# Routing of the batches earlier, scatters given out by step, late layer norms on VectorE, and the maxima turned at the end of a step

## The chip, the cores and the metric

One core of a Trainium2 chip runs the whole program. The metric is the device time of one execution in microseconds (us). Engines are named as in the profile: PE (matrix products), DVE (vector), ACT (activations), POOL (GpSimd), SP (the queue that issues most transfers).

## The reference, cut to what matters

Eight batches of 256 tokens with 256 features go through one cross-attention layer (16 heads of 16 features) and one mixture-of-experts layer (8 experts, hidden size 1024, two experts for each token), in float32:

```python
x = x + xattn(layernorm(x), ctx, ctx, Wq, Wk, Wv, Wo, bo, masks)     # softmax(q k' / 4) v, then Wo
z = layernorm(x)
gate = softmax(z @ w_gate.T);  two largest per token, their weights in cw
h = gelu(einsum('td,edh->teh', z, W1) + b1)
x = x + einsum('ted,te->td', einsum('teh,ehd->ted', h, W2) + b2, cw)
```

The kernel computes an expert only for the tokens that chose it. It writes each token's normalised row twice, into the lists of its two experts, and later works through these lists.

## The kernel before, in words

**Steps.** All engines run the same list of steps, s = -16 to 99, each engine its own part of each step in a fixed order. Nothing but semaphores ties the engines together, so "step" is an order on each engine and no clock. Step s takes one pair of heads (m = s mod 8) of batch n = s div 8 through the first score product: `scores_for_max(s)` on PE, then the row maxima `nmax` on DVE (`take_max`, L863). Ten steps later the same pair is multiplied again with the maximum subtracted (`scores(s - 10)`, L1341) and exponentiated on ACT (L1143); `weighted` (L1353) multiplies two such pairs by the values in every other step. So the 64 instructions L863 lie in steps 0 to 63 and the 64 instructions L1143 in steps 10 to 73. In this way rows of the trace are given step numbers here.

**The table of due steps.** What happens once per batch hangs on names in a table `due[s]`: for the back of the attention `div`, `divide`, `ao`, `aT`, `o`, `add`, then the second layer norm `ln2` (statistics, DVE), `norm2` (POOL: the power -0.5 of the variance, `inverse_deviation`, L554, and the two normalising instructions, L565), `y` (four turns on PE), `yT` (ACT). The routing follows in six groups of batches, (0, 1), (2, 3), 4, 5, 6 and 7: `logits` (PE), `choose` (DVE), `gate_exp` (ACT), `gates`, `tags` (DVE), `count` (PE), `places`, `rows` (DVE) and `scatter` (POOL). A scatter is one indirect DMA (L575) for each half batch and each of two choices: eight for a group of two batches and four for one of one. `total` (PE) sums the counts after groups 3, 4 and 5, and `lists_of` (DVE) makes the table of tiles from it. POOL's `scatter` waits for the group's `rows` and `tags` and then issues its DMAs without another wait.

**The maxima.** Row maxima of one batch are put together on DVE in step 8n+7 (`maxima`), turned on PE at the very start of step 8n+8 (`turn_maxima`, L1294), copied by ACT to `mT` (L1102) and sent by ACT's DMA queue (L1124) into the operand of `scores`. In ACT's own order `maxima_out` is the first thing of step 8n+8, ahead of that step's exponential.

**The experts.** From step 76 on each step also holds a unit, a quarter of a tile. 23 tiles (16 of 256 rows, 7 of 128) are worked through: gather of the rows, two weight matrices of 1 MB each, split in two parts by ACT and DVE, 48 + 48 products for a full tile on PE, the scaled sum on DVE and an indirect add to the output on POOL (L534). SP loads a tile's rows (`xg`) and weights in `sp_tile`; tiles 0 and 1 are loaded in step 71, behind the first table and behind the landings of the scatters of groups 0 to 3. After step 99 the units go on by themselves.

## Time and profile before

| what | value |
|---|---|
| median of 3 runs | 527.25 us (525.56 to 530.07) |
| the profiled execution | 525.33 us, of which the span from first to last instruction is 524.0 us |
| PE busy | 457.9 us, 87% of the span |
| DVE, ACT, POOL busy | 69%, 64%, 32% |
| mean granted PE clock | 0.94 of full |

The page shows shares of the whole span. The kernel has quite different stages, though: attention at an even pace up to about 177 us, a mixed stage to about 241 us, and the experts from there to the end. What matters is read from the stage in question.

### The profile page before, as it was taken

Reading aid. Unit: us, or ns where it says so; the run is one execution under the profiler, and the core shown is the slowest. Engines: PE = TensorE matmul, PEld = TensorE weight load, DVE = VectorE, ACT = ScalarE, POOL = GpSimd, SP = SyncE. Lnnn points to the kernel's source line nnn. Section 1 sums busy time; section 2 is a strip of 40 time slices with the busy share of each in tenths; the row PEclk is TensorE's granted clock in tenths of the full one; section 3 lists DMA queues with packets and bytes.
Section 4 is the critical chain, followed back from the end, with each engine's and each line's share of the span. In section 5 each row is a group of like instructions: output and inputs, shape, how many; then the busy total and the mean of one; then the engine's idle time right before and its main releaser. Section 6 shows DMA issues by size and latency. Waiting matters only on the chain.

```text
span 524.0 us, 10489 instructions
## 1 busy us (share of the span) xinstructions
PE 457.9 (87%) x3741; PEld 390.5 (75%) x3741; DVE 360.4 (69%) x791; ACT 334.8 (64%) x569; POOL 165.2 (32%) x213
## 2 busy tenths in 40 slices
PE   4897989999999844658889987999999999999993
PEld 3365666766765622427889977899999999999992
DVE  3276776776777751336977997298868788888862
ACT  1123776667666522335968856498779889889880
POOL 6023330352321577210361513132333213312323
PEclk9999999999999966665989989899999999999998
DMA  6557615324310023149275859859787987878822
GB/s 226 175 159 218 210 62 171 124 69 150 124 66 24 31 95 106 42 164 357 83 246 176 278 154 269 254 206 270 218 242 240 277 250 232 276 266 245 282 32 30
DMA packets 44356, 93.03 MB, mean 178 GB/s; under 512 B 6928, under 2 KB 30096, under 8 KB 38416
## 3 DMA queue, kind: packets, MB, share of 16 engines
q1 hardware_dynamic: 35072, 81.41, 46.3%
q0 software_dynamic: 7152, 9.46, 9.3%
q10 hardware_dynamic: 2080, 1.49, 0.9%
q8 instruction: 31, 0.51, 0.4%
q14 instruction: 21, 0.17, 0.1%
HBM read 63.01 MB, written 14.26 MB: 147 GB/s over the span
## 4 chain that ended last, share of the span: by engine, by line
PE 52%; issue 10%; DVE 10%; ACT 9%; DMA 6%; POOL 4%; another core or an unknown queue 4%; SPq 3%; ACTq 1%; DVEq 0%; POOLq 0%
PE S L1218 13%; PE bank L1233 12%; PE bank L1278 6%; PE bank L1286 5%; PE S L1318 4%; DMA w_in<-in_W 4%; PE bank L1353 3%; DVE nmax L863 3%; ACT hf L1068 2%; PE S L1391 2%; PE bank L1270 2%; PE S L1341 2%; ACT W2p L1049 2%; ACT Q L1037 1%
## 5 line engine op out<-in xcount | busy, mean ns | idle before, releaser
L1218 PE MATMUL S<-xgT,Q 128*128 128x256 f32 (+1 forms) x736 | 139.1, 289 | 8.7 <-DVE xgT L757 5.2
L534 POOL DMA_INDIRECT out<-y,slot x39 | 69.4, 1780 | 177.3 <-DVE y L781 103.7
L1218 PEld LDWEIGHTS S<-xgT,Q 128*128 128x128 f32 x736 | 117.5, 198 | 9.3 <-issue 9.3
L863 DVE TENSOR_REDUCE nmax<-S 128x4 f32<-128x1024 f32 x64 | 78.4, 1225 | 47.6 <-PE S L1318 45.1
L1218 PE MATMUL S<-xgT,K 128*128 128x256 f32 (+1 forms) x368 | 105.6, 287 | 0.0
L1068 ACT ACTIVATE hf<-S,b1c 128x256 f32<-128x256 f32 (+1 forms) x184 | 70.6, 435 | 40.2 <-PE S L1218 36.4
L1143 ACT ACTIVATE prob<-S 128x1024 f32<-128x1024 f32 x64 | 65.8, 1028 | 38.8 <-PE S L1341 27.7
L767 DVE TENSOR_TENSOR hp<-hf,hp 128x512 fp32r<-128x512 f32 (+1 forms) x92 | 55.8, 607 | 29.7 <-ACT hp L1081 29.3
L1218 PEld LDWEIGHTS S<-xgT,K 128*128 128x128 f32 x368 | 72.6, 197 | 0.0
L734 DVE TENSOR_TENSOR K<-w_in,Q 128x1024 fp32r<-128x1024 f32 x46 | 56.4, 1225 | 19.9 <-ACT Q L1037 19.9
L1233 PE MATMUL bank<-W2p,hp 128*128 128x256 f32 x528 | 67.6, 284 | 0.3 <-DVE y L777 0.3
L1233 PEld LDWEIGHTS bank<-W2p,hp 128*128 128x128 f32 x528 | 64.7, 191 | 0.6 <-issue 0.4
L554 POOL TENSOR_TENSOR rstd<-ve,half 128x2 f32<-128x2 f32 x16 | 11.8, 736 | 137.7 <-DVE ve L848 137.3
L1081 ACT ACTIVATE hp<-hf 128x512 fp32r<-128x512 f32 (+1 forms) x92 | 52.3, 569 | 2.9
L1037 ACT ACTIVATE Q<-w_in 128x1024 fp32r<-128x1024 f32 x46 | 48.2, 1048 | 8.6 <-DMA w_in<-in_W 7.5
L1233 PE MATMUL bank<-Q,hp 128*128 128x256 f32 x272 | 51.3, 282 | 1.3 <-DVE y L777 1.2
L1233 PEld LDWEIGHTS bank<-Q,hp 128*128 128x128 f32 x272 | 42.9, 188 | 1.6 <-issue 1.6
L575 POOL DMA_INDIRECT lists<-x2n,rows x32 | 31.7, 990 | 39.3 <-DVE rows L965 31.1
L1353 PE MATMUL bank<-prob,V 128*32 128x256 f32 x512 | 37.7, 416 | 1.2 <-ACT prob L1143 1.2
L1233 PE MATMUL bank<-K,hp 128*128 128x256 f32 x136 | 38.3, 282 | 0.0
L1318 PEld LDWEIGHTS S<-K,Q 64*128 64x128 f32 x256 | 19.1, 184 | 24.8 <-issue 13.2
L1318 PE MATMUL S<-K,Q 64*128 64x256 f32 x256 | 32.2, 330 | 5.7 <-DVE nmax L863 5.1
(179 smaller groups left out, 702.1 us busy)
## 6 DMA issues: line engine op xcount, KB each, us to landing
w_in<-in_W SPq DMA_DIRECT2D x46, 1024.0 KB, 7.9
K<-flat_k SPq DMA_DIRECT2D x24, 256.0 KB, 2.4
Q<-flat_q SPq DMA_DIRECT2D x24, 256.0 KB
xg<-lists SPq DMA_DIRECT2D x16, 265.0 KB
b_in<-in_b SPq DMA_DIRECT2D x23, 128.0 KB
lists<-zero SPq DMA_DIRECT2D x9, 265.0 KB, 4.9
cin<-in_ctxT SPq DMA_DIRECT2D x8, 256.0 KB, 3.5
xin<-in_x SPq DMA_DIRECT2D x8, 256.0 KB, 3.9
```

The source lines that it names most:

```text
L534: st_y[i % 4].after(pool.indirect_dma_start(out=out, out_offset=bass.IndirectOffsetOnAxis(ap=slot[i % 4][:, t:t + 1], axis=0), in_=y[i % 2 ...
L734: w1_lo.after(dve.tensor_tensor(W1p[i % 2][1][:, c], w1_in[i % 2][:, c], W1p[i % 2][0][:, c].bitcast(F32), ALU.subtract))
L767: h_lo.after(dve.tensor_tensor(hp[i % 2][1][:, c, 0:n], hf[pair % 2][:, :, 0:n], hp[i % 2][0][:, c, 0:n].bitcast(F32), ALU.subtract))
L863: max_done.after(dve.tensor_reduce(nmax[n % 4][:, :, :, m].rearrange("p t r -> p r t"), S1[:].rearrange("p r (t k) -> p r t k", t=TT), AX. ...
L1037: w1_hi.after(act.activation(W1p[i % 2][0][:, c], w1_in[i % 2][:, c], ACT.Copy))
L1068: h_act.after(act.activation(hf[pair % 2][:, u, 0:n], h_bank[pair][:, u, 0:n], ACT.Gelu, bias=b1c[i % 3][:, 2 * pair + u:2 * pair + u + 1]))
L1081: h_hi.after(act.activation(hp[i % 2][0][:, 2 * pair:2 * pair + 2, 0:n], hf[pair % 2][:, :, 0:n], ACT.Copy))
L1143: exp_done.after(act.activation(prob[s % 4][:].rearrange("p r t l -> p (r t l)"), S2[:].rearrange("p r l -> p (r l)"), ACT.Exp, scale=SCALE))
L1218: ins = pe.matmul(h_bank[pair][:, u, 0:n], W1p[k][a][:, kc, m * P:(m + 1) * P], xgT[k][c][:, kc, 0:n], start=(j == 0), stop=(j == len(term ...
L1233: ins = pe.matmul(y_bank[:, t, :], hp[k][a][:, m, t * P:(t + 1) * P], W2p[k][c][:, m, :], start=(j == 0), stop=(j == len(terms) - 1))
L1318: i = pe.matmul(S1[:, r, t * L:(t + 1) * L], Q[n % HELD][a, m, t * P:(t + 1) * P], K[n % HELD][a, m, :], start=not masked, stop=(not maske ...
L1353: i = pe.matmul(b[j * OS:(j + 1) * OS, 0:L], V[n % 3][:, t, r * MP + m, :], prob[(MP * n + m) % 4][:, r, t, :], start=(t == 0), stop=(t == ...
```

## The change

- `ROUTE` now gives each group its own steps. Group 0: `rows` in step 51, 60 before. Group 1: `rows` in 61, 63 before. Group 2: 64, 65 before. Group 3: 68, 69 before. Group 4: 78, 77 before. Group 5 keeps 89. In the early groups a DVE part that reads a PE result stands one step behind it (`count` 59, `places` 60), where before both could be in one step.
- `scatter` no longer stands in the table: `SCATTERS` gives each group a first step and a number of DMAs for each step (1 for group 0, 2 for groups 1, 2 and 4, 4 for groups 3 and 5). Only the first DMA of a group waits.
- Batches 3 to 7 have their two normalising instructions of the second layer norm on DVE, under a due name of their own, `norm_dve`; before, DVE had them only for batch 6. POOL keeps `inverse_deviation`.
- `turn_maxima` stands behind `scores_for_max`, `scores`, `div` and `weighted` of its step on PE. ACT's order isn't changed.
- `total` of stage 0 and the loads of tiles 0 and 1 are one step sooner (69 and 70).

```diff
+    ON_DVE = 3
+    SCATTERS = {0: (51, 1), 1: (61, 2), 2: (65, 2), 3: (69, 4), 4: (78, 2), 5: (90, 4)}
-    ROUTE = dict(logits=38, choose=39, gate_exp=40, gates=42, tags=46, count=50, places=51, rows=52, scatter=54)
     LATE_BACK = {
-        4: dict(div=52, divide=53, ao=54, aT=55, o=57, add=58, store=59, ln2=59, norm2=59, y=61, yT=62),
-        5: dict(div=59, divide=59, ao=60, aT=61, o=61, add=62, store=63, ln2=62, norm2=63, y=64, yT=65),
-        6: dict(div=67, divide=67, ao=68, aT=69, o=69, add=70, store=71, ln2=71, norm2=71, y=72, yT=73),
-        7: dict(div=77, divide=77, ao=79, aT=79, o=81, add=81, store=83, ln2=81, norm2=82, y=84, yT=84)}
-    LATE_ROUTE = {
-        1: dict(logits=60, choose=60, gate_exp=61, gates=62, tags=62, count=62, places=62, rows=63, scatter=63),
-        2: dict(logits=63, choose=63, gate_exp=64, gates=65, tags=65, count=65, places=65, rows=65, scatter=66),
-        3: dict(logits=66, choose=66, gate_exp=67, gates=68, tags=68, count=68, places=69, rows=69, scatter=70),
-        4: dict(logits=74, choose=74, gate_exp=75, gates=76, tags=76, count=76, places=76, rows=77, scatter=78),
-        5: dict(logits=86, choose=86, gate_exp=88, gates=88, tags=88, count=89, places=89, rows=89, scatter=90)}
-    LISTED = {0: (3, 70), 1: (4, 79), 2: (5, 92)}
+        3: dict(div=44, divide=45, ao=46, aT=47, o=50, add=51, store=53, ln2=52, norm2=52, norm_dve=53, y=54, yT=55),
+        4: dict(div=52, divide=53, ao=54, aT=55, o=56, add=57, store=59, ln2=57, norm2=57, norm_dve=58, y=59, yT=60),
+        5: dict(div=59, divide=60, ao=61, aT=61, o=62, add=63, store=64, ln2=63, norm2=63, norm_dve=64, y=65, yT=65),
+        6: dict(div=67, divide=67, ao=68, aT=69, o=69, add=70, store=71, ln2=70, norm2=70, norm_dve=71, y=73, yT=74),
+        7: dict(div=77, divide=77, ao=79, aT=79, o=81, add=81, store=83, ln2=81, norm2=82, norm_dve=82, y=84, yT=84)}
+    ROUTE = {
+        0: dict(logits=45, choose=46, gate_exp=47, gates=48, tags=48, count=49, places=50, rows=51),
+        1: dict(logits=56, choose=57, gate_exp=58, gates=59, tags=59, count=59, places=60, rows=61),
+        2: dict(logits=61, choose=62, gate_exp=63, gates=63, tags=63, count=63, places=64, rows=64),
+        3: dict(logits=66, choose=66, gate_exp=67, gates=68, tags=68, count=68, places=68, rows=68),
+        4: dict(logits=75, choose=75, gate_exp=76, gates=76, tags=76, count=77, places=77, rows=78),
+        5: dict(logits=86, choose=86, gate_exp=88, gates=88, tags=88, count=89, places=89, rows=89)}
+    LISTED = {0: (3, 69), 1: (4, 79), 2: (5, 92)}
...
-        SP_TILES = {71: (0, 1), 76: (2,), 79: (3,), 82: (4,), 86: (5,), 90: (6,)}
+        SP_TILES = {70: (0, 1), 76: (2,), 79: (3,), 82: (4,), 86: (5,), 90: (6,)}
...
-                    if now["norm2"] != NB - 2:
+                    if now["norm2"] < ON_DVE:
                         normalise(1, now["norm2"])
-                if "scatter" in now:
-                    scatter(now["scatter"])
+                for i, (first_step, each) in SCATTERS.items():
+                    for k in range(each):
+                        scatter(i, (s - first_step) * each + k)
...
+                if "norm_dve" in now:
+                    normalise(1, now["norm_dve"])
...
-                if "mx" in now:
-                    turn_maxima(now["mx"])
                 if 0 <= s < NP:
                     scores_for_max(s)
                 if 0 <= s - LAG < NP:
@@ -1412,6 +1415,8 @@
                 n, m = divmod(s - LAG - 2, MP)
                 if 0 <= n < NB and m % 2 == 0:
                     weighted(n, m // 2)
+                if "mx" in now:
+                    turn_maxima(now["mx"])
```

## Rows read from the trace of the kernel before

**Rows 1.** Table of stretches of the span: busy time, granted clock, DMA share.

```profile
101.40:122.10 20.70, 20.05 (x184) 13.93 (x183) 15.11 (x30) 14.23 (x21) 7.66 (x8) 1.00 0.36 121
...
204.00:236.00 32.00, 17.01 (x122) 9.86 (x122) 9.54 (x52) 10.02 (x16) 9.82 (x11) 0.61 0.29 105
...
270.00:274.00 4.00, 4.00 (x23) 4.00 (x22) 1.28 (x4) 2.72 (x5) 2.55 (x2) 0.57 0.91 280
```

**Rows 2.** Timeline: exponentials of steps 60 and 69, first expert product.

```profile
175.44 1.03 ACT L1143 ACTIVATE prob<-S 128x1024 f32<-128x1024 f32 x1 [0.80 <-PE S L1341]
...
219.76 1.02 ACT L1143 ACTIVATE prob<-S 128x1024 f32<-128x1024 f32 x1
...
241.74 0.77 PE L1218 MATMUL S<-xgT,Q 128*128 128x256 f32 x2 [1.73 <-DVE xgT L757]
```

**Rows 3.** Chain that ended last, 177 to 242 us: four of its pieces.

```profile
185.40 4.19 another core or an unknown queue
...
198.79 4.33 another core or an unknown queue
...
204.17 8.87 another core or an unknown queue
...
222.65 2.52 another core or an unknown queue
```

**Rows 4.** Timeline of group 0's first scatter, steps 62 and 63, and of steps 66 and 67.

```profile
181.00 1.23 POOL L575 DMA_INDIRECT lists<-x2n,rows  x1 [0.34 <-DVE rows L965]
...
185.14 0.50 PE L1318 MATMUL S<-K,Q 64*128 64x256 f32 x4
...
192.52 1.02 ACT L1143 ACTIVATE prob<-S 128x1024 f32<-128x1024 f32 x1 [6.83 <-remote]
...
201.38 1.19 PE L1370 MATMUL bank<-WgT,yT 128*128 128x8 f32 x8
...
213.16 0.17 DVE L917 TENSOR_SCALAR gate<-bank 128x16 f32<-128x16 f32 x1 [11.70 <-remote]
```

**Rows 5.** Timeline: last scatter of the second run, and group 4's last.

```profile
209.82 0.96 POOL L575 DMA_INDIRECT lists<-x2n,rows  x1 [0.30 <-issue]
...
254.36 0.97 POOL L575 DMA_INDIRECT lists<-x2n,rows  x1 [0.31 <-issue]
```

**Rows 6.** Timeline of step 32, in which the maxima of batch 3 are turned.

```profile
101.72 0.38 PE L1294 MATMUL bank<-ident,mrep 128*32 128x128 f32 x2
...
102.19 0.38 ACT L1102 ACTIVATE mT<-bank 32x256 f32<-32x256 f32 x1 [1.17 <-PE bank L1294]
...
102.60 0.64 ACTq L1124 DMA_DIRECT2D Q<-mT  x1
102.70 1.07 PE L1353 MATMUL bank<-prob,V 128*32 128x256 f32 x16
...
103.34 1.03 ACT L1143 ACTIVATE prob<-S 128x1024 f32<-128x1024 f32 x1 [0.77 <-PE S L1341]
...
105.67 1.99 PE L1278 MATMUL bank<-xT,WqT 128*128 128x256 f32 x8 [0.65 <-ACT xT L1102]
```

**Rows 7.** Timeline: normalising of batches 4, 6 and 7.

```profile
180.72 0.66 PE L1270 MATMUL bank<-ident,x2n 128*128 128x128 f32 x4 [1.28 <-POOL x2n L565]
...
230.66 0.74 DVE L854 TENSOR_SCALAR x2n<-x,mv,rstd 128x256 f32<-128x256 f32 x2 [0.94 <-POOL rstd L554]
...
264.25 4.75 POOL L565 TENSOR_SCALAR x2n<-x,mv,rstd 128x256 f32<-128x256 f32 x2
...
269.05 0.66 PE L1270 MATMUL bank<-ident,x2n 128*128 128x128 f32 x4 [1.90 <-POOL x2n L565]
```

**Rows 8.** Timeline: group 3's rows, total 0, and the first load of rows.

```profile
219.06 0.16 DVE L965 TENSOR_REDUCE rows<-off 128x2 int32<-128x16 f32 x1
...
223.28 0.18 PE L1395 MATMUL bank<-run,onesb 128*128 128x8 bf16 x1
...
230.30 0.41 SPq L383 DMA_DIRECT2D xg<-lists  x1
```

More of the change, by code:

```diff
@@ L136, in build @@
             due[LATE_BACK[n][name] if n in LATE_BACK else MP * n + o][name] = n
+        if n in LATE_BACK:
+            due[LATE_BACK[n]["norm_dve"]]["norm_dve"] = n
     for i, ns in enumerate(GROUPS):
-        for name, o in ROUTE.items():
-            due[LATE_ROUTE[i][name] if i in LATE_ROUTE else MP * ns[-1] + o][name] = i
+        for name, step in ROUTE[i].items():
+            due[step][name] = i
     for stage, (i, step) in LISTED.items():
@@ L559, in normalise @@
                     pool.wait_ge(pe_misc.sem, filled_by("xn", n - 1))
-                if which and n >= KEPT:
-                    pool.wait_ge(pe_misc.sem, filled_by("y", n - KEPT))
-                    pool.wait_ge(st_list[n % KEPT].sem, 16 * TT * TOP * (n // KEPT))
                 for t in range(TT):
@@ L566, in normalise, with scatter @@
                                                            ALU.subtract, ALU.mult))
-            def scatter(i):
+            def scatter(i, d):
                 ns = GROUPS[i]
-                pool.wait_ge(rows_done.sem, 2 * (i + 1))
-                pool.wait_ge(x2n_tag.sem, 2 * (i + 1))
-                for u, n in enumerate(ns):
-                    for t in range(TT):
-                        for k in range(TOP):
-                            st_list[n % KEPT].after(pool.indirect_dma_start(
-                                out=lists, out_offset=bass.IndirectOffsetOnAxis(
-                                    ap=rows[i % 2][:, k, u * TT + t:u * TT + t + 1], axis=0),
-                                in_=x2n[:, n % KEPT, t], in_offset=None))
+                if not 0 <= d < len(ns) * TT * TOP:
+                    return
+                u, t, k = d // (TT * TOP), d // TOP % TT, d % TOP
+                if d == 0:
+                    pool.wait_ge(rows_done.sem, 2 * (i + 1))
+                    pool.wait_ge(x2n_tag.sem, 2 * (i + 1))
+                n = ns[u]
+                st_list[n % KEPT].after(pool.indirect_dma_start(
+                    out=lists, out_offset=bass.IndirectOffsetOnAxis(
+                        ap=rows[i % 2][:, k, u * TT + t:u * TT + t + 1], axis=0),
+                    in_=x2n[:, n % KEPT, t], in_offset=None))
             pool_r.after(pool.memset(taken[:], 0.0))
@@ L851, in normalise @@
                 dve.wait_ge(ln_rstd[which].sem, n + 1)
+                if which and n >= KEPT:
+                    dve.wait_ge(pe_misc.sem, filled_by("y", n - KEPT))
+                    dve.wait_ge(st_list[n % KEPT].sem, 16 * TT * TOP * (n // KEPT))
                 for t in range(TT):
@@ L993, in dve_attention @@
                     statistics(1, now["ln2"])
-                    if now["ln2"] == NB - 2:
-                        n = now["ln2"]
-                        dve.wait_ge(pe_misc.sem, filled_by("y", n - KEPT))
-                        dve.wait_ge(st_list[n % KEPT].sem, 16 * TT * TOP * (n // KEPT))
-                        normalise(1, n)
+                if "norm_dve" in now:
+                    normalise(1, now["norm_dve"])
                 if "ln1" in now:
```

## The prediction

> **What bounds the kernel now.** I read the table of stretches first, since the page's shares mix three stages. In attention at its even pace eight steps take 20.7 us, and PE is busy in 20.05 of them at the full clock (2.4 GHz) [rows 1]: PE bounds it, and what holds PE there costs its full length. Between 204 and 236 us no engine is busy for much more than half the time and the mean granted clock is 0.61, mostly the lower level (1.2 GHz) [rows 1]. In the timeline steps 60 to 69 take 219.76 - 175.44 = 44.3 us, 4.9 us each, where 2.6 was the pace, and the first expert product starts at 241.74 [rows 2]. From there on tile follows tile; SP, POOL and DVE do their parts unit by unit, so what starts the first tile sooner ends the kernel sooner by the same.
>
> The chain of waits tells what stretches steps 60 to 73: four pieces that it puts down to no engine of this core, 4.19, 4.33, 8.87 and 2.52 us, 19.9 in all [rows 3]. The timeline is to be read for what PE had done by then. PE's products of step 63 are recorded from 185.14 on, yet the exponential fed by them starts at 192.52; the logits of group 3 are recorded at 201.38, yet DVE reads them at 213.16, after 11.70 us of waiting [rows 4]. So PE's completions arrive late, not its work. In that time POOL issues scatters back to back, 0.96 us each with 0.30 between: eight from 181.00 on, to 191.1, and twelve up to 209.82 + 0.96 = 210.8 [rows 4, 5]. The late completions come from about the fourth scatter of a run on, and stop some 1 to 2.5 us after its last. The four of group 4, ending at 255.3 [rows 5], hold nobody. I take the length of a run of scatters as the cause; the trace shows only that they go together. A page would allow the lateness itself: the Trainium skill (Perfetto Trace Analysis, Tensor Engine Instruction) says that a product's recorded end is estimated and that its semaphore goes out only when PSUM has acknowledged the bytes.
>
> Counted against the pace of the neighbouring steps, the lateness costs 4.3 us in the run of eight (steps 62 to 64), 9.6 in the run of twelve (64 to 67) and 1.5 in group 3's four: 15.4 of the 19.9, because other work went on beside it.
>
> **The change part by part.**
>
> Maxima turned at the end of the step. Removed: 0.31 us of PE ahead of the scores. But ACT copies the turned maxima first in its step, and its exponential comes behind. In step 32 now: turn at 101.72, copy at 102.19 (0.47 later, 0.38 long), DMA issue at 102.60 for 0.64, exponential at 103.34 [rows 6]. With the change the turn stands behind `weighted`, which would start 0.33 sooner, at 102.37, and takes 1.00: turn at 103.37, copy 103.85, issue 104.27, exponential 105.0. That is 1.66 us later. PE needs this exponential for the next scores, and the turned rows that ACT copies behind it for the q products at 105.67, for which it waits 0.65 already [rows 6]. Between them it has only 0.7 us of other work. So PE loses 1.66 us in each of steps 16, 24, 32, 40 and 48, and perhaps 0.5 in step 56, where 3.9 us of `o` and `logits` products fill the hole: +8.8. Nothing gives this back, as PE bounds the stage. Ends: 0 (if DVE or the queue order hides all of it) and 6 x 1.66 = 10.
>
> Routing sooner. Its work isn't less, only moved: of group 1's some 2.9 us of DVE and 1.9 of PE (the same instructions in the timeline before) leave steps 60 to 63 for 56 to 60. Beside PE-bound steps it is paid there and saved later: 0. Its ends are -2 and +3 us: at best PE's holes hide it, at worst DVE becomes the bound of 57 and 58.
>
> DVE readers one step behind. When PE's completion is late by less than a step, DVE no longer stands still with `nmax` queued behind the reader; but the scores wait on late completions all the same. I take -1 us; ends 0 and -3.
>
> Scatters given out. Here the code decides: POOL has no clock of steps. After the first DMA of a group only other waits of POOL's part them. Group 0: one, then the wait for `ln2` of batch 3, then five in a row, then that of batch 4, then two. Group 1: four, the wait for `ln2` of batch 5 in step 63, then four; group 2's `rows` (step 64) are ready before these end (4 x 1.26 = 5 us, two steps), so its four follow at once: a run of eight. Group 3: four. In place of 8, 12 and 4 the runs are 5, 2, 4, 8 and 4. Priced as now, a run of four at 1.5 to 2, of five 2.5 (it has one scatter beyond the fourth), of eight 4.3: 2.5 + 2 + 4.3 = 8.8 ahead of group 3's, where 4.3 + 9.6 = 13.9 are lost now: -5.1. Ends: -13.9 (no run is late) and 0.
>
> Norms on DVE. For batches 3, 4, 5 and 7 DVE gets 0.74 us and POOL loses 2.4 or more. The wait of PE for batch 4, 1.28 us [rows 7], goes: -1.3. Batch 7: POOL took 4.75 us, and PE stood 1.90 [rows 7]; the clock then fell and was 0.57 in the next 4 us [rows 1], worth 1.7 (half of the 3.4 us at the lower level). Next due is DVE, whose order has two units' work ahead, so both go: -3.6; ends -2 and -4.5. If DVE were the bound there, its 0.74 would come back. The added wait is DVE's for `rstd`: behind it in step 64 stands `nmax` of no further step, but `choose` and `rows`; behind it in 58 `nmax` of step 59. POOL's `inverse_deviation` stands behind up to five scatters, 6.3 us. By the order above these are issued before DVE has the variance; I take 0, the other end is the last rival.
>
> First table a step sooner. From group 3's `rows` (219.06) to the load of its tile's rows (230.30) are 11.2 us now [rows 8]. The scatters take 4 x 1.26 = 5.0 and land about 2 us later, 7 in all; the table's small DVE instructions and SP's register loads take 230.30 - 223.28 = 7.0 behind `total`, which came 4.2 behind `rows` [rows 8] and with its step brought forward can come right behind them. So 7.2 in place of 11.2: -4.0. Ends -5 and -1. The 11.4 us from this load to the first product [rows 2, 8] stay (5.0 of them are the weights' transfer), and the exponentials of steps 69 to 73 fit beside them at 2.6 each.
>
> Clock. PE is busy for 17.0 us between 204 and 236 at a mean clock of 0.61 [rows 1]; at the full clock the same products would take 10.4. With fewer holes part of these 6.6 us comes back, but much of it lies beside waits: I take -1.5, ends 0 and -4.
>
> Group 4 and 5, and the store of batch 6 that now stands behind two tile loads on SP, end beside the experts: 0.
>
> **Sum**, against the profiled execution: 8.8 - 1.0 - 5.1 - 1.3 - 3.6 - 4.0 - 1.5 = -7.7, so 525.3 - 7.7 = 517.6 us. This execution lies 1.9 below the median of the runs and 0.2 below their lowest; I put the median at 519.
>
> **Rivals.**
>
> The runs don't stall at all any more, since none but one is longer than five. For it: group 4's four cost nothing. Against: the run of eight is left. It gives 519 - 8.8 = 510.
>
> The maxima cost nothing. Against it speaks that ACT's order has no way round. For it: PE's record ends are modelled, and its 97% may hide slack that takes up 1.7 us in each eight steps. It gives 510 as well, and 501 with the first.
>
> The scatters are not the cause, or each costs the same 0.64 us (15.4 / 24) however it is dealt: the change doesn't do what it says. All 13.9 us stay: 519 + 5.1 = 524, or with the other gains at their weak ends 526. The Trainium skill (SBUF — State Buffer, two separate sides) has a rule for this: PE's port waits for nobody, and transfers and engine ports don't contend. By that rule scatters could not hold PE; rows 4 show them together, and nothing else that would.
>
> Slower: DVE waits for POOL. `norm_dve` of batches 4, 5 and 6 needs `rstd`, which POOL computes only when its scatters ahead are issued, and all of DVE's queue stands behind. It decides from the point where a group's `rows` come less than 5.0 us (four scatters) before `ln2` of the next batch; group 1's are due two steps, 5.5 us, before. Once each with 5 us, and with the stalls as they are now: 519 + 5.1 + 2 x 5 = 534.
>
> **How the numbers follow.** Forecast, 519 (513 to 523): 0.45. No stalls, 510: 0.17. Free maxima, 510 or less: 0.13. Stalls unchanged, 524 to 526: 0.15. DVE behind POOL, 534: 0.10. The range takes both cases of 510 with part of what lies below, and those of 524 to 526 with 1 us more: 503 to 527. Changes under 1% (5.3 us) can hardly be told from none with this kernel, whose runs differ by 4.5 us. Faster by more (under 522): four fifths of the first case and the next two, 0.66; slower (over 532.5): 0.10; the rest, 0.24, is the same.
>
> **What would show it.** In the attention stage eight steps should take 22.3 us and the exponential of step 32 start 3.3 us after the turn's old place. Runs of scatters in the timeline: 1, 5, 2, 4, 8, 4. The pieces of the chain without an engine should add up to some 10 us, the largest in the run of eight. From group 3's `rows` to the load 7 us; first product at about 235 to 238; no fall of the clock at batch 7's turns. I am wrong if the even stage keeps 20.7 us (maxima), if late completions appear without POOL's scatters or stay away in the run of eight, or if DVE idles before L854 for several us.

## The result and the profile after

The changed kernel takes 545.38 us (median of 4 runs, 544.59 to 546.95); the kernel before took 527.62 us beside it (525.56 to 530.07). The ratio is 1.037 (95% interval 1.032 to 1.042): slower by 18 us, where 8 us less were forecast. The profiled execution took 544.59 us, its span is 543.3 us; lines after L150 stand 4 to 8 further down than before. The page of the changed kernel, busy time and granted clock in 40 slices of 13.6 us:

```profile
PE 470.4 (87%) x3741; PEld 399.2 (73%) x3741; DVE 363.1 (67%) x799; ACT 333.7 (61%) x569; POOL 155.4 (29%) x205
...
PE   4898898998978878775799988599999999999993
...
PEclk9999998989899866667799999799999999999998
```

PE's share of the span is the 87% of before, but that is 470.4 us busy in place of 457.9 for the same 3741 instructions, which last longer at the lower clock. The clock's line of the page of the kernel before, in slices of 13.1 us, for comparison:

```profile
PEclk9999999999999966665989989899999999999998
```

Now the clock falls again and again from slice 7 on, and from 186 to 248 us its mean is 0.61. The same in the table of stretches (busy time of PE, PEld, DVE, ACT and POOL with counts, granted clock, DMA share, GB/s): first the eight steps from the exponential of step 24 to that of step 32, then two pieces of step 32, then about steps 57 to 73.

```profile
84.30:107.80 23.50, 21.33 (x178) 14.60 (x178) 15.22 (x30) 13.59 (x20) 4.81 (x6) 0.93 0.33 107
107.80:111.20 3.40, 1.56 (x9) 1.25 (x10) 0.91 (x1) 3.19 (x5) 2.85 (x3) 1.00 0.12 26
111.20:114.60 3.40, 3.40 (x21) 2.10 (x23) 0.95 (x1) 1.12 (x2) 0.00 (x0) 0.51 0.00 0
...
186.00:248.00 62.00, 48.88 (x332) 32.88 (x332) 30.37 (x121) 22.19 (x33) 19.58 (x21) 0.61 0.19 64
```

Steps 24 to 32 now take 23.50 us; the same steps took 20.33 before (exponentials at 83.01 and 103.34). The cause is in the timeline of step 32 (start, duration, engine, line; in brackets the wait ahead and who ended it), which answers to [rows 6]:

```profile
106.18 0.39 PE L1299 MATMUL bank<-ident,mrep 128*32 128x128 f32 x2
...
106.67 0.37 ACT L1107 ACTIVATE mT<-bank 32x256 f32<-32x256 f32 x1 [2.95 <-PE bank L1299]
...
107.81 1.02 ACT L1148 ACTIVATE prob<-S 128x1024 f32<-128x1024 f32 x1 [0.77 <-ACT mT L1107]
...
108.89 0.50 PE L1346 MATMUL S<-Q,K 64*128 64x256 f32 x4 [1.45 <-ACT prob L1148]
...
110.14 2.31 PE L1283 MATMUL bank<-xT,WqT 128*128 128x256 f32 x7 [0.75 <-ACT xT L1107]
```

ACT stands still for 2.95 us until PE has turned the maxima; the exponential comes 1.14 us behind the copy, and PE waits for it (1.45) and again for the turned rows (0.75). Then comes what I had not counted: from 111.2 to 114.6 us the granted clock is at the lower level (0.51, so 1.2 of 2.4 GHz), and eight q products whose records took 1.99 us [rows 6] last from 110.14 to about 112.8 (the last row shows seven of the eight). The clock falls so in steps 24, 32 and 40. In step 16 PE has the same two waits, 1.45 and 0.75 us, and the q products still take 2.00 us: no fall there. From exponential to exponential each of the four turns costs 1.77 us (step 32 comes 5.11 behind step 31, where it was 3.34), and each of the three falls 1.4 to 1.6 more: 4 x 1.77 + 4.5 = 11.6 us.

The chain's pieces without an engine, 19.9 us in [rows 3], are down to two:

```profile
225.96 2.38 another core or an unknown queue
228.38 2.85 another core or an unknown queue
```

And from group 3's rows to the load of the first tile's rows and to the first product, which answers to [rows 8] and the last of [rows 2]:

```profile
236.96 0.16 DVE L973 TENSOR_REDUCE rows<-off 128x2 int32<-128x16 f32 x1
...
244.11 0.41 SPq L388 DMA_DIRECT2D xg<-lists  x1
...
257.21 0.77 PE L1223 MATMUL S<-xgT,Q 128*128 128x256 f32 x2 [4.09 <-DVE xgT L762]
```

7.15 us where 11.24 were, but then 13.1 to the product in place of 11.4.

The two kernels by stage, cut at the starts of exponentials, at the first expert product and at DVE's split of the fifth tile's rows (tile 4; L757, now L762), us. The right half is a later series of runs (last experiments), in which the kernel before took only 512.8 us:

| stage | before | changed | difference | before, later | changed, later | difference |
|---|---|---|---|---|---|---|
| to step 15 | 60.06 | 57.81 | -2.3 | 59.81 | 58.91 | -0.9 |
| 15 to 45 | 76.62 | 88.22 | +11.6 | 76.59 | 88.25 | +11.7 |
| 45 to 54 | 24.58 | 28.94 | +4.4 | 26.25 | 28.93 | +2.7 |
| 54 to 62 | 22.56 | 34.86 | +12.3 | 25.17 | 34.43 | +9.3 |
| 62 to 72 | 43.35 | 35.48 | -7.9 | 25.02 | 31.38 | +6.4 |
| 72 to first product | 14.57 | 11.90 | -2.7 | 16.10 | 14.74 | -1.4 |
| to tile 4 | 51.17 | 52.15 | +1.0 | 49.49 | 52.16 | +2.7 |
| to the end of the span | 231.09 | 233.94 | +2.9 | 230.87 | 231.40 | +0.5 |
| span | 524.0 | 543.3 | +19.3 | 509.3 | 540.2 | +30.9 |

The stage to step 15 lasted 57.5 to 60.1 us in all traces whatever the kernel, and single stages between 45 and 72 shift by 1.5 to 2.5 us among kernels that do the same work there; smaller differences mean nothing. The last stage too lasted 230.3 to 233.0 us among kernels with the expert code of before. The 25.02 of steps 62 to 72 is the lowest of its kind: the kernels of runs 11, 13 and 14, with the same work there or nearly so, took 28.5 to 29.7 in the later series, and 22.0 to 23.5 in steps 54 to 62, where this trace has 25.17.

### The profile page after: what moved, and what is told of

It reads as the page before. It is cut to its first block, busy times and chain, and to the rows that moved or that the text cites. A ratio compares the mean times of both kernels' runs of the same rounds, so it can differ in the third digit from the quotient of the medians.

```text
span 543.3 us, 10488 instructions
## 1 busy us (share of the span) xinstructions
PE 470.4 (87%) x3741; PEld 399.2 (73%) x3741; DVE 363.1 (67%) x799; ACT 333.7 (61%) x569; POOL 155.4 (29%) x205
## 4 chain that ended last, share of the span: by engine, by line
PE 60%; DVE 11%; ACT 10%; issue 8%; DMA 5%; SPq 2%; POOL 2%; another core or an unknown queue 1%; ACTq 1%; DVEq 0%; POOLq 0%
PE S L1223 16%; PE bank L1238 13%; PE bank L1283 6%; PE bank L1291 5%; PE bank L1358 5%; PE S L1323 5%; DVE nmax L871 3%; DMA w_in<-in_W 3%; PE S L1346 3%; ACT hf L1073 2%; PE S L1396 2%; PE bank L1275 2%; ACT Q L1042 2%; ACT prob L1148 1%; PE bank L1375 1%
## 5 line engine op out<-in xcount | busy, mean ns | idle before, releaser
L1223 PEld LDWEIGHTS S<-xgT,Q 128*128 128x128 f32 x736 | 116.5, 196 | 12.4 <-issue 12.3
L539 POOL DMA_INDIRECT out<-y,slot x39 | 71.5, 1833 | 179.1 <-DVE y L786 92.1
L1042 ACT ACTIVATE Q<-w_in 128x1024 fp32r<-128x1024 f32 x46 | 48.1, 1046 | 13.6 <-DMA w_in<-in_W 13.5
L1086 ACT ACTIVATE hp<-hf 128x512 fp32r<-128x512 f32 (+1 forms) x92 | 52.2, 567 | 2.9
L1346 PE MATMUL S<-Q,K 64*128 64x256 f32 x256 | 31.3, 327 | 16.3 <-ACT prob L1148 14.4
L1323 PEld LDWEIGHTS S<-K,Q 64*128 64x128 f32 x256 | 21.0, 202 | 31.9 <-issue 16.1
L1323 PE MATMUL S<-K,Q 64*128 64x256 f32 x256 | 34.7, 352 | 10.7 <-DVE nmax L871 10.4
L1358 PE MATMUL bank<-prob,V 128*32 128x256 f32 x512 | 39.0, 428 | 2.5 <-DVE ao L900 1.9
```

What stands on the lines that cost most here:

```text
L539: st_y[i % 4].after(pool.indirect_dma_start(out=out, out_offset=bass.IndirectOffsetOnAxis(ap=slot[i % 4][:, t:t + 1], axis=0), in_=y[i % 2 ...
L1042: w1_hi.after(act.activation(W1p[i % 2][0][:, c], w1_in[i % 2][:, c], ACT.Copy))
L1086: h_hi.after(act.activation(hp[i % 2][0][:, 2 * pair:2 * pair + 2, 0:n], hf[pair % 2][:, :, 0:n], ACT.Copy))
L1223: ins = pe.matmul(h_bank[pair][:, u, 0:n], W1p[k][a][:, kc, m * P:(m + 1) * P], xgT[k][c][:, kc, 0:n], start=(j == 0), stop=(j == len(term ...
L1323: i = pe.matmul(S1[:, r, t * L:(t + 1) * L], Q[n % HELD][a, m, t * P:(t + 1) * P], K[n % HELD][a, m, :], start=not masked, stop=(not maske ...
L1358: i = pe.matmul(b[j * OS:(j + 1) * OS, 0:L], V[n % 3][:, t, r * MP + m, :], prob[(MP * n + m) % 4][:, r, t, :], start=(t == 0), stop=(t == ...
```

## The experiments

"On before" and "on changed" say which kernel was edited. Times are medians, the ratio is to the kernel before in the same series. There are four series of four runs each, and each ran on another chip: runs 1 to 4 on number 0, 5 to 8 on 10, 9 to 12 on 15 and 13 to 16 on 5. A piece of the chain without an engine is a wait for something that the profile can't name; a single instruction's wait of this kind is marked `remote`.

**1. Maxima at the start again, on changed.** The call of `turn_maxima(now["mx"])` moved back ahead of the scores.

> The changed kernel with one part undone: the maxima are turned at the start of their step on PE again. Theory M (the turn's place costs all of the loss, because ACT's exponential waits behind the copy, PE stands still and its clock falls in each batch): eight steps take 20.7 us again instead of 24, the exponential of step 60 comes near 183 us instead of 200.5, and the time is 520 to 527. Theory R (the routing steps and the norms on DVE cost it): the time stays above 538, and steps 48 to 60 stay slow.

529.92 us, 1.010 (1.005 to 1.016): 15.5 us less than the changed kernel. Stage 15 to 45 is 76.61 us again. But 54 to 62 stays at 33.3 us, where before had 22.6: a second loss that has nothing to do with the maxima.

**2. Maxima at the end alone, on before.**

```diff
-                if "mx" in now:
-                    turn_maxima(now["mx"])
                 if 0 <= s < NP:
...
                     weighted(n, m // 2)
+                if "mx" in now:
+                    turn_maxima(now["mx"])
```

> The kernel before with one part of the change alone: the maxima are turned behind the weighted sums of their step. Theory M: 3.3 us lost in each of five steps and some in step 56, the exponential of step 60 at 192 instead of 175, a time of 540 to 547. Forecast of the prediction for this part: +8.8, so 536. Theory R: no more than 3 us above the kernel before.

539.29 us, 1.027 (1.021 to 1.033), +14.5 us; 15 to 45 takes 88.56 us, so 11.9 more for four batches: 3.0 each on average, of which 1.77 is the wait; the clock falls behind steps 24, 32, 40 and 56, not behind 16 and 48. Step 56 pays the full 1.78 as well. From both sides the late turn costs about 15 us.

**3. ACT's exponential first, on changed.** `maxima_out` put behind `exponentials` on ACT; PE still turns late.

> The changed kernel with the maxima still turned at the end of the step on PE, but ACT takes its copy of them behind the step's exponential instead of ahead of it. Theory M with ACT's order as the mechanism: PE no longer waits for the exponential, eight steps take 20.4 to 21 us, the time is within 3 us of the kernel with the turn at the start (520 to 527). If PE's own order is what costs (the bank, or the later transfer of the maxima), the time stays above 535.

534.92 us, 1.019 (1.014 to 1.024). Stage 15 to 45 takes 79.80 us: of the 11.6 us there 8.4 are gone. Step 32 there:

```profile
102.12 1.02 ACT L1148 ACTIVATE prob<-S 128x1024 f32<-128x1024 f32 x1 [1.57 <-PE S L1346]
...
103.01 0.39 PE L1299 MATMUL bank<-ident,mrep 128*32 128x128 f32 x2
...
103.50 0.37 ACT L1107 ACTIVATE mT<-bank 32x256 f32<-32x256 f32 x1 [0.35 <-PE bank L1299]
...
105.35 0.60 ACT L1107 ACTIVATE xT<-bank 128x512 f32<-128x512 f32 x1
...
106.00 1.99 PE L1283 MATMUL bank<-xT,WqT 128*128 128x256 f32 x8 [1.50 <-ACT xT L1107]
```

The exponential waits for its scores alone, the q products take 1.99 us again, and the clock is granted in full (1.00) from step 16 to 45; what is left, 0.8 us for each batch, is PE's 1.50 for the turned rows, where it waited 0.65 [rows 6]. ACT's order is the main mechanism, and the fall of the clock behind it carries a good part of the price. The time stays 5.0 us above run 1, though, and not within the 3 that I had expected: besides the 3.2 of this stage, steps 45 to 54 take 29.29 in place of 27.62, with a fall of the clock behind step 48.

**4. Scatters spaced out, on before.** Each scatter of groups 0 to 2 waits until the one before has landed.

```diff
                         for k in range(TOP):
+                            if i < 3:
+                                pool.wait_ge(st_list[n % KEPT].sem, st_list[n % KEPT].value)
```

> The kernel before, but each scatter of groups 0 to 2 waits on POOL until the one before has landed, so one comes every 3 us or so instead of every 1.26. Theory D (PE's completions come late because scatters are issued back to back): the pieces without an engine in the chain between 180 and 215 us (17.4 us before) fall under 4, and steps 62 to 67 take under 22 us instead of 33.8; the time is 512 to 527, the gain being eaten in part by later landings of the lists. Theory N (each scatter costs 0.64 us however it is spaced, or something else holds PE): the pieces add up to 10 or more again.

545.55 us, 1.039 (1.034 to 1.044). Not one piece of the chain is without an engine and no wait is `remote`, so PE's completions are in time when the scatters stand apart; run 2, on the same chip with the scatters as before, has 20.8 us of such pieces. The price is another one: POOL's queue blocks. The list of waits (engine, line, waited for; us in all, times, longest), 196 to 250 us:

```profile
POOL lists L575 <- DMA lists<-x2n,rows: 27.7, 15, 2.1
...
PE bank L1272 <- DVE x2n L856: 19.2, 1, 19.2
...
PE bank L1272 <- POOL x2n L565: 16.1, 1, 16.1
```

The norms behind the scatters on POOL come late and PE stands for 19.2 and 16.1 us. It says nothing of what the stalls are worth.

**5. Late norms on DVE, on before** (batches 3, 4, 5 and 7 at steps 57, 60, 63 and 82).

```diff
+    for n, step in {3: 57, 4: 60, 5: 63, 6: 71, 7: 82}.items():
+        due[step]["norm_dve"] = n
...
-                    if now["norm2"] != NB - 2:
+                    if now["norm2"] < 3:
                         normalise(1, now["norm2"])
...
```

> The kernel before with one part alone: batches 3 to 7 have their second layer norm's normalising on DVE, at steps 57, 60, 63, 71 and 82; routing, scatters and maxima as before. The prediction has -1.3 for batch 4 and -3.6 for batch 7: 4.9 us off, about 520 against 525. The rival (DVE waits behind POOL's scatters for the power, with the next maxima queued behind it) expects no gain or a loss of up to 5 us: in step 63 DVE has to wait for POOL, which is issuing eight scatters.

520.65 us, 0.988 (0.980 to 0.996), -5.0 us by the medians, with an interval of about -2 to -10: the fastest of this series. The first product to tile 4 takes 47.37 us in place of 51.17. Part of this isn't the norms' own: the 51.17 holds the fall of the clock at 270 us. Of seven traces with batch 7's norm on POOL and group 4 where it was, two have such a fall (this one and run 4, 51.17 and 51.01); the other five take 49.5 to 50.0 there. DVE waits for `rstd` 1.04 us once, in batch 5.

**6. Scatters in a lump, on changed, maxima at the start.** `SCATTERS = {0: (62, 8), 1: (63, 8), 2: (66, 4), 3: (69, 4), 4: (78, 4), 5: (90, 4)}`.

> The changed kernel with the maxima at the start again and the scatters not given out early: group 0's eight come in step 62 in a row, group 1's eight in 63, group 2's four in 66, group 3's four in 69, with the routing steps as changed. Theory C (the scatters that fell into the PE-bound stage cost more than they saved, because the late completions stop PE there and its clock falls before step 60): steps 48 to 60 take 29 to 31 us instead of 40.3, and the late completions come back after step 62; the time is 518 to 530. Theory W (the routing work itself is what makes steps 48 to 60 slow): they stay at 37 us or more.

532.58 us, 1.012 (1.003 to 1.021), 2.8 us over run 7 of the same series. With runs of 8 and 12 again the chain has only 5.9 us without an engine, but the chain shows too little here: single waits marked `remote` sum to 10.3 us on ACT and 9.7 on DVE, where run 1 has 5.8 and 2.7 and the kernel before 19.1 and 18.5. So the lumps bring part of the lateness back. Steps 54 to 62 take 33.7 us as in run 1. That doesn't clear the scatters: POOL was ahead, group 0's eight ran from 178.2 to 188.3 us, beside the exponentials of steps 58 to 60, and two late completions lie there:

```profile
186.72 1.23 DVE L871 TENSOR_REDUCE nmax<-S 128x4 f32<-128x1024 f32 x1 [3.90 <-remote]
...
188.15 1.02 ACT L1148 ACTIVATE prob<-S 128x1024 f32<-128x1024 f32 x1 [3.57 <-remote]
```

Run 16 settles it: no completion is late there, and these steps take 34.4 us, some 1.5 of it for the late turn. The second loss does not need late completions.

**7. Scatters truly tied to steps, on changed, maxima at the start.** Ahead of each later share of a group POOL waits for `s2_done` of the step.

> The changed kernel with the maxima at the start again, and the scatters of groups 0 to 2 tied to their steps: from a group's second step on POOL waits until the score products of the step before are done. Group 0 then has one scatter every 2.5 us. Theory D (lateness needs scatters back to back): no late completions between 160 and 172 us, where 5 us of chain pieces without an engine or waits for one stood, and steps 48 to 60 take 30 to 33 us instead of 40.3; 518 to 525 in all. Theory N (each scatter costs the same): steps 48 to 60 stay at 38 us or more.

529.75 us, 1.006 (1.002 to 1.011); by the stages as run 1. The waits had mostly been met when POOL came to them, and group 0's scatters still start some 1.3 us apart. It tells nothing of spacing.

**8. First table a step sooner, on before** (group 3's places, rows, scatters, `LISTED` and `SP_TILES` a step sooner).

> The kernel before with one part alone: places and rows of group 3 in step 68, its scatters and the first table in 69, the loads of tiles 0 and 1 in 70. The prediction's term: from group 3's rows to the load 7.2 us instead of 11.2, so 521 against 525. If what stands behind the load (the weights, or the steps up to 76) is what sets the first product, the time stays within 1 us.

524.65 us, 0.995 (0.991 to 0.999): -2.5 us by this ratio, -1.0 by the medians, so a small gain at most. Rows to load fell from 11.2 to 7.2 us, load to first product rose from 11.4 to 13.3.

The next eight ran in two series in which the kernel before took 512.27 and 512.81 us, 12 to 15 less than so far: their times in the expectations are to be read as differences.

**9. Routing of groups 1 and 2 back, on changed, maxima at the start.**

```diff
-    SCATTERS = {0: (51, 1), 1: (61, 2), 2: (65, 2), 3: (69, 4), 4: (78, 2), 5: (90, 4)}
+    SCATTERS = {0: (51, 1), 1: (63, 8), 2: (66, 4), 3: (69, 4), 4: (78, 2), 5: (90, 4)}
...
-        1: dict(logits=56, choose=57, gate_exp=58, gates=59, tags=59, count=59, places=60, rows=61),
-        2: dict(logits=61, choose=62, gate_exp=63, gates=63, tags=63, count=63, places=64, rows=64),
+        1: dict(logits=60, choose=60, gate_exp=61, gates=62, tags=62, count=62, places=62, rows=63),
+        2: dict(logits=63, choose=63, gate_exp=64, gates=65, tags=65, count=65, places=65, rows=65),
...
```

> The changed kernel with the maxima turned at the start and with the routing of groups 1 and 2 (and their scatters) put back to the steps that it had before: norms on DVE, the first table a step sooner and the scatters of groups 4 and 5 dealt out stay. Theory A, the routing of group 1 (two batches) on PE and DVE in steps 56 to 61 is what makes steps 48 to 60 last 40 us in place of 28.7: they fall to 29 to 31 us, steps 60 to 69 grow from 36.2 to 42 to 43 us (as with the norms alone), and the span comes out some 3 to 8 us under the 528.6 of the run without the maxima: 520 to 525. Rival B, the back parts of batches 3 to 5 that the change also moved in these steps (output product, addition, norm) do it: steps 48 to 60 stay at 37 to 40 us and the time at 528 or more.

522.13 us, 1.022 (1.014 to 1.029). Steps 54 to 62 take 25.90 us in place of 33.30, where kernels without the moves take 22.0 to 25.2. Steps 48 to 60, by which I had meant to judge, still take 36.8: they end amid a step that is long in one kernel and short in the other, and were a bad measure. By what was written down neither theory came out: steps 48 to 60 didn't fall to A's 29 to 31, and the time is 10 us over before, where A's 520 to 525 meant 0 to 5 under the 525 that the kernel before then took; B's 37 to 40 us and 3 or more over it were nearly met. What the run does show is the place: steps 54 to 62 lose 7.4 us when groups 1 and 2 go back, though run 1, with which I compare, is of another series. The rest is left: 45 to 54 has +3 and the first product to tile 4 takes 52.2 us. An estimate for the whole: the changed kernel is 29.2 us over before where completions aren't late (run 16), without the late turn (15) it would be some 14 over, and this one is 9.9 over, so putting groups 1 and 2 back gives about 4 us.

**10. Routing of groups 0 and 1 sooner alone, on before** (with batch 3's back part, which it needs).

> The kernel before with the routing of groups 0 and 1 alone moved sooner (group 0 to steps 45 to 51, group 1 to 56 to 61, with the back part of batch 3 that it needs), norms on GpSimd, scatters as before. Theory A: steps 48 to 60 last 36 us or more in place of 28.7, 60 to 69 gives part of it back (44.3 falls to 36 to 40), in all 0 to 6 us slower than before: 525 to 531. Rival B, it is the back parts of batches 4 and 5 and the norms on DVE in these steps: steps 48 to 60 stay under 32 us and the time falls by what 60 to 69 gives back, to 517 to 521.

517.61 us, 1.012 (1.007 to 1.017), +5.3 us by the medians, +6 by the ratio. Steps 54 to 58 take 13.7 us in place of 9.8, steps 48 to 60 33.7: between the two theories. Three things move here. Group 0 alone costs nothing that can be measured (run 14), and batch 3's back part about 1.4 us in steps 49 to 52 (9.5 where run 14 has 8.1), so some 3 to 4 us are left for group 1; no run moves it by itself. That the back parts of batches 4 and 5 in the same steps make it dearer, as the 33.3 us of run 1 suggest, wasn't run alone either.

**11. Norms on DVE and first table sooner together, on before.**

> The kernel before with the two parts together that gained alone: late norms on DVE (5.0 us alone) and the first table a step sooner (2.5 us alone). If they add up: 517 to 519. If both only bring the lists forward and what stands behind them (the last steps before the first unit) sets the end: 519 to 521, as the norms alone.

510.46 us, 0.996 (0.994 to 0.999): -1.8 us here. The norms give their part, 47.37 us to tile 4 (49.49 in run 15). The table gives almost nothing: from group 3's rows to the load are 9.5 us, where run 8 has 7.2 and run 15 10.2. The steps are faster here, so POOL's scatters are what is waited for. Sixteen go out back to back, the last of them starts at 213.67 us, the table is complete at 210.4, and the load comes at 216.43. And DVE, with all its queue, waits twice for POOL's power of the variance, which comes behind the scatters, as the last rival of the prediction had it: 3.63 us at 191.84, behind a run of eight, and here behind the sixteen:

```profile
215.52 0.74 DVE L856 TENSOR_SCALAR x2n<-x,mv,rstd 128x256 f32<-128x256 f32 x2 [3.23 <-POOL rstd L556]
```

Behind tile 4 it takes 232.57 us where run 15 has 230.87; run 14, with the expert code of before, takes 232.96, so that difference says nothing. It is the fastest kernel of these series, as run 5 was of the first; both beat both kernels, by little.

**12. The same with PE turning late and ACT's exponential first.**

> The same as the kernel with norms on DVE and the first table sooner, with the maxima turned at the end of their step on PE, and ScalarE's copy of them put behind its exponential. Theory A, the loss from the late turn is ScalarE's order alone (its exponential queued behind the copy): then this costs nothing beside the kernel with the two parts, 0 plus or minus 2 us. Rival B, the late turn also delays the masked maxima and with them the next batch's query product, or PE's order itself costs: 4 us slower or more.

513.99 us, 1.003 (1.000 to 1.006), 3.5 us over run 11. Stage 15 to 45 takes 79.81 us against 76.62. The 0.8 us for each batch of run 3 stand confirmed, away from the rest of the change: even with ACT's order mended the late turn gains nothing.

**13. Group 4's routing a step later alone, on before** (the changed kernel has it so).

```diff
-        4: dict(logits=74, choose=74, gate_exp=75, gates=76, tags=76, count=76, places=76, rows=77, scatter=78),
+        4: dict(logits=75, choose=75, gate_exp=76, gates=76, tags=76, count=77, places=77, rows=78, scatter=78),
```

> The kernel before with group 4's routing alone one step later, as in the changed kernel (logits and choice in step 75, counts and places in 77, rows in 78). Theory A, PE's count of step 77 stands behind the first unit's products in PE's queue and waits for the choice, which on DVE comes behind the split of the weights and batch 7's division: the stretch from the first unit's first product to the fifth table (tile 4) grows from 51 to 54 to 56 us and the kernel is 3 to 6 us slower than before. Rival B, the 5 us of that stretch come from another of the moves (batch 6's or 7's norm on DVE): 0 plus or minus 1.5 us.

518.37 us, 1.011 (1.007 to 1.015), +5.6 us, as theory A had it; the first product to tile 4 takes 54.26 us in place of 49.49. Its timeline behind the first unit's first products:

```profile
236.03 0.75 DVE L892 TENSOR_TENSOR ao<-bank,rden 128x256 f32<-128x256 f32 x2
236.60 0.17 PE L1385 MATMUL bank<-chosen,before 128*128 128x8 bf16 x1 [3.09 <-DVE ao L892]
...
236.73 0.77 PE L1218 MATMUL S<-xgT,Q 128*128 128x256 f32 x2
```

The counts of step 77, on PE, use a bank that DVE's division of batch 7 must have read first, and DVE comes to that only behind the split of a weight. PE stands 3.09 us with unit 1's products queued behind, and two products still take 0.77 us, their time at the lower clock.

**14. Group 0's routing sooner alone, on before** (steps 45 to 51, scatters still in 62).

> The kernel before with group 0's routing alone sooner (steps 45 to 51 in place of 46 to 60; its scatters stay in step 62). Theory A, the gates, tags, counts and places of group 0 then stand ahead of the row maxima on DVE in steps 46 to 51: steps 45 to 54 grow by 3 us (27.6 in place of 24.6), steps 57 to 60 fall by nothing, and the kernel is 2 to 4 us slower. Rival B, it is batch 3's back part that costs these 3 us: 0 plus or minus 1.5 us.

513.22 us, 1.000 (0.997 to 1.003): nothing, within 1.7 us. Steps 45 to 54 take 26.22 us; with group 0 where it was they take 24.58 (run 13) or 26.25 (run 15). In runs 9 and 10 batch 3's back part was moved as well: the exponential of step 51 comes 4.4 us behind that of 50 in both, and 2.3 here.

**15. The kernel before again.**

> The kernel before, unchanged, for its trace beside the others of this call. If the late completions of PE belong to the kernel: the chain has 15 us or more without an engine between 185 and 225 us, and the time is 525 to 530. If they belong to the chip that it runs on: under 3 us of them, steps 60 to 69 last 31 to 34 us in place of 44, and the time is 510 to 514. The ratio is 1 within 0.4% either way.

513.61 us, 1.001 (0.997 to 1.004). The chain from 145 to 270 us has no piece without an engine. The exponentials of steps 60 and 69, which answer to [rows 2]:

```profile
176.83 1.02 ACT L1143 ACTIVATE prob<-S 128x1024 f32<-128x1024 f32 x1 [0.79 <-PE S L1341]
...
206.97 1.02 ACT L1143 ACTIVATE prob<-S 128x1024 f32<-128x1024 f32 x1
```

30.1 us where 44.3 were, in the same program. And the scatters still ran back to back, eight from 182.38 to 191.50 and sixteen from 195.94 to 215.04. So close scatters alone don't make PE's completions late. By what I had written down the lateness belongs to the chip: the traces of the first result and of the chips 0 and 10 show it wherever eight or more scatters go out in a row, none of the eight traces from the chips 15 and 5 shows it. No chip was used in two series, so the chip and the time of the run aren't told apart. The gain between the two series lies in this stretch: steps 62 to 72 are 18.3 us shorter, those from 45 to 62 4.3 longer.

**16. The changed kernel again.**

> The changed kernel, unchanged, in the same call. Where the late completions do not appear, the change cannot win anything from them, and it loses more: the maxima 14.5, group 0 3, group 1 and the back parts 8 to 12, group 4 5, less 6 for the norms and the table: 22 to 28 us over the kernel before (ratio 1.045 to 1.055). Where they do appear, 17 to 20 us as in the first result (1.037).

541.97 us, 1.056 (1.051 to 1.062): +29 us, no late completion either. The list of waits of steps 54 to 62 in this run (first fence) and in run 15 (second):

```profile
DVE nmax L871 <- PE S L1323: 14.7, 7, 6.5
...
ACT prob L1148 <- PE S L1346: 7.8, 4, 3.6
...
PEld S L1323 <- DVE nmax L871: 4.0, 3, 2.5
```

```profile
DVE nmax L863 <- PE S L1318: 6.6, 4, 4.2
...
ACT prob L1143 <- PE S L1341: 3.4, 4, 1.5
```

DVE waits for PE and PE for DVE in turn. What each does meanwhile is in the timeline of the first trace of the changed kernel, steps 57 and 58:

```profile
185.63 2.54 PE L1375 MATMUL bank<-WgT,yT 128*128 128x8 f32 x14 [1.35 <-ACT V L1107]
...
189.36 1.23 DVE L871 TENSOR_REDUCE nmax<-S 128x4 f32<-128x1024 f32 x1 [6.97 <-PE S L1323]
...
190.50 0.68 DVE L909 TENSOR_TENSOR x<-bank,x 128x512 f32<-128x512 f32 x1
...
193.95 0.18 DVE L935 TENSOR_SCALAR chosen<-rank 128x32 bf16<-128x32 f32 x1
194.05 1.22 DVE L871 TENSOR_REDUCE nmax<-S 128x4 f32<-128x1024 f32 x1
...
195.32 0.80 PE L1323 MATMUL S<-K,Q 64*128 64x256 f32 x4 [1.59 <-DVE nmax L871]
```

Group 1's logits (two batches) stand ahead of PE's scores, so DVE idles for 6.97 us. Then its addition, statistics and choice, 190.50 to 194.13, stand ahead of the next row maxima, so PE waits 1.59. The stage runs at a granted clock of 0.66 in this series, where the kernel before has 0.86 (and 1.00 in its first trace, in 22.6 us):

```profile
176.10:210.50 34.40, 27.79 (x212) 20.19 (x208) 19.33 (x51) 12.58 (x20) 9.43 (x10) 0.66 0.13 45
```

```profile
162.60:187.80 25.20, 23.72 (x212) 17.06 (x211) 17.08 (x45) 12.86 (x20) 10.48 (x11) 0.86 0.09 29
```

The 212 matrix instructions of each are busy 4.1 us longer, which is the clock, and PE is idle 5.1 us longer, which are the waits.

## Why the prediction was wrong

The sign was wrong. By its own steps:

- **Maxima, +8.8 us with ends 0 and 10.** The mechanism is as written: ACT's copy first, the exponential behind it, PE waiting for it and for the turned rows, and each maxima step nearly as late as the arithmetic said (1.77 us for 1.66). The size was off: 14.5 (run 2) to 15.5 (run 1). Two things are missing in the sum. Behind four of the six turns in run 2 (three of the four in the even stage) the clock was at its lower level for 3.4 us, which cost 1.4 to 1.6 us more; my end of 10 left no room for it. The row for it was there, in another place: 0.57 behind batch 7's wait of 1.90 [rows 1, 7]. And step 56, put at 0.5, cost 1.78 in run 2 and, with the clock, 1.5 in the changed kernel (34.86 for 33.30 in steps 54 to 62).
- **Routing sooner, 0 with ends -2 and +3.** This step failed outright. Steps 45 to 62 lose 13.8 us without the late turn (run 1 against before: 3.0 and 10.7; waits of 2.7 and 1.8 us for late completions, beside scatters moved into these steps, are in it). Group 1 has a part in it: 7.4 us of steps 54 to 62 go when groups 1 and 2 go back (run 9), and groups 0 and 1 with batch 3's back part cost 5 to 6 (run 10), of which group 0 has nothing (run 14) and the back part about 1.4. Run 16 shows that late completions aren't needed for it. How the rest divides among group 1, group 2 and the back parts of batches 4 and 5 stays open. I had counted instructions, which are the same, and not that each waits in an ordered queue ahead of `scores` on PE and `nmax` on DVE, which wait for each other in every step. The reversed case, "DVE the bound of 57 and 58", was priced at DVE's surplus instead of at two idle engines and a lower clock.
- **Group 4, 0.** Not looked at: +5.6 us alone (run 13). "End beside the experts" was true of its scatters, not of its counts on PE.
- **Norms on DVE, -4.9.** -5.0 in run 5 by the medians, and that is in part luck: 2.0 us of it lie ahead of step 15, which the norms don't touch, and up to 1.7 is the fall of the clock behind batch 7, which I had taken as given and which two of seven such traces show. The feared wait of DVE for POOL's `rstd` was 0.8 us once in the changed kernel; it did come in run 11, 3.63 and 3.23 us, behind eight and sixteen scatters in a row.
- **First table, -4.0.** The place is right to 0.1 us (7.1 for 7.2). But 1.9 of it come back before the first product, as ACT and DVE have attention's last steps and the weights ahead of the table's rows: -2.5 by the ratio in run 8, -1.0 by the medians. I had let the 11.4 us behind the load stay.
- **Scatters, -5.1, and DVE readers, -1.** Steps 62 to 72 fell by 7.9 us and the pieces without an engine from 19.9 to 5.2, under the 10 I forecast; the scatters ran 1, 5, 2, 4, 8 and 4 in a row as the code had told, and both late pieces lie at the end of the run of eight. Between the series the kernel before gains 14.8 us and the changed one 3.4: against late completions the change was worth 11.4 us, more than forecast, but where there are none it pays 6.4 in the same steps against run 15, and 1.7 to 2.9 against runs 11, 13 and 14. The cause that I gave has its part but is not enough. Scatters far apart leave none late (run 4) and lumps bring part of it back (run 6), but the kernel before has none at all in run 15, nor has the run of eight in run 16, which was one of my signs of being wrong. What else is needed stays open; the traces say only that it came on some chips and not on others.
- **Clock, -1.5.** The wrong way: the mean over the span fell from 0.940 to 0.923.

For the first result the parts sum to +14.5 for the maxima, +13.8 and +5.6 for the moved steps, -5.0 and -2.5 for norms and table, -7.9 for steps 62 to 72: +18.5, and 17.8 were measured. The agreement is better than the parts deserve, since some were measured alone and some in company, some are stages and some whole times, and the -2.5 is -1.0 by the medians: that it comes so close is luck.

The rule of the Trainium skill that I held against late completions (SBUF — State Buffer, two separate sides) agrees with runs 9 to 16 and not with the 19.9 us of [rows 3], nor with run 4, where they go when the scatters are spaced. Which way scatters reach PE's completions, if not by a port, no run here shows.

## What to carry to other kernels

Where two engines hand each other work in every step (here scores to row maxima to scores), an instruction moved ahead of either hand-over can cost its length on both engines, and then the clock that the hole costs: price a moved step at each queue's hand-over, not by busy time. Waits of TensorE can cost more than their length: here 1.45 and 0.75 us in one step were followed by a stretch at the lower clock that cost 1.4 to 1.6 us, but not every time, and a single wait of 1.50 us mostly by none. Such a stretch belongs into the upper end of a range. Before a gain is built on a stall, look whether the stall is there on another chip and in another series of runs of the same kernel.

## What the runs showed of the hardware

- Behind waits of PE of 1.45 and 0.75 us in one step the granted clock fell to 0.51 for 3.4 us in steps 24, 32 and 40 of the changed kernel and not in step 16; where only one wait of 1.50 us was left (run 3), it stayed at 1.00 in all four and the q products took 1.99 us.
- One program took 527.6, 524.8 (chip 0) and 525.6 us (chip 10) in three series and 512.3 (chip 15) and 512.8 us (chip 5) in two others, each within 1.4% in itself. The difference lies mostly where completions of PE came up to 8.9 us late in the first and not at all in the last.
- With late completions absent the same change reads 1.056 in place of 1.037: a ratio of two kernels measured on one chip need not hold on the next.
- With eight and with sixteen scatters ahead of it in POOL's queue, one every 1.26 us, a 0.7 us instruction of POOL came so late that DVE waited 3.63 and 3.23 us for it (run 11).
